# The normalisation of the early groups, dealt out one small piece per step, in two stages of an eight-stage network on one core

## The reference

```python
x = x + _layernorm(_L0_attn_ref(_layernorm(x, axis=-1), ...), axis=-1)   # linear attention, 16 heads
x = x + _layernorm(_L0_ffn_ref(_layernorm(x, axis=-1), ...), axis=-1)
...
x = x + _layernorm(_L2_attn_ref(_layernorm(x, axis=-1), ...), axis=-1)   # causal softmax attention, 16 heads
x = x + _layernorm(_L2_ffn_ref(_layernorm(x, axis=-1), ...), axis=-1)
```

## Time and profile before

| | |
|---|---|
| median of 3 runs | 3116.63 us (3113.25 to 3116.71) |
| the profiled execution | 3116.61 us, span 3114.8 us |
| mean granted TensorE clock | 0.935 of full speed |
| busy: PE | 2705.1 us, 87% of the span |
| busy: DVE | 2057.1 us, 66% |
| busy: ACT | 1571.8 us, 50% |
| busy: POOL | 1074.1 us, 34% |

### The profile page before, as it was taken

How to read it: one execution, slowest core, us unless ns; L and a number is a source line. 1 busy time by engine, 2 the same in 40 slices (tenths; PEclk the granted TensorE clock), 3 DMA queues, 4 the chain that set the end, 5 groups by cost and what they waited for, 6 DMA issues and landing times. The chain is left out here.

```text
span 3114.8 us, 55189 instructions
## 1 busy us (share of the span) xinstructions
PE 2705.1 (87%) x21256; PEld 1691.7 (54%) x21276; DVE 2057.1 (66%) x4308; ACT 1571.8 (50%) x3080; POOL 1074.1 (34%) x784
## 2 busy tenths in 40 slices
PE   8995899989899799998999798798877899777698
PEld 5552455567676566665567566465643334335465
DVE  5758999945644665647554665466548999996554
ACT  4334688862423444444544555365457676643122
POOL 3201000001143344434443444154227777773000
PEclk9995899989899899999999899998999999998899
DMA  1000000001120200000000000000013344340000
GB/s 55 1 4 1 2 3 3 3 2 61 49 92 22 84 1 1 1 1 1 1 1 1 29 1 1 1 1 1 1 52 135 136 143 143 137 141 27 1 1 14
DMA packets 34228, 105.41 MB, mean 34 GB/s; under 512 B 3456, under 2 KB 14592, under 8 KB 33200
## 3 DMA queue, kind: packets, MB, share of 16 engines
q1 hardware_dynamic: 31952, 97.69, 9.0%
q0 software_dynamic: 2016, 4.19, 0.4%
HBM read 94.01 MB, written 7.86 MB: 33 GB/s over the span
## 5 line engine op out<-in xcount | busy, mean ns | idle before, releaser
L2082 POOL TENSOR_TENSOR many_probs<-many_probs,many_rinv 128x2048 f32<-128x2048 f32 (+7 forms) x128 | 269.8, 2107 | 371.6 <-DVE many_rinv L2121 371.6
L1062 DVE TENSOR_REDUCE heads_halfmax<-heads_qmajor 128x1 f32<-128x512 f32 x512 | 316.4, 681 | 32.8 <-PE heads_qmajor L923 29.4
L3477 DVE TENSOR_TENSOR_SCAN stream_state<-stream_decay,stream_state 128x512 f32<-128x512 f32 x256 | 306.3, 1233 | 0.8 <-ACT stream_decay L3309 0.5
L1027 ACT ACTIVATE weights<-heads_kmajor 128x1024 f32<-128x1024 f32 x256 | 259.3, 1027 | 71.7 <-PE heads_kmajor L935 66.3
L2051 ACT ACTIVATE many_probs<-many_score,many_negmax 128x1024 f32<-128x1024 f32 (+7 forms) x256 | 187.4, 737 | 179.7 <-DVE many_negmax L2105 175.9
L2105 DVE TENSOR_REDUCE many_negmax<-many_score 128x1 f32<-128x1024 f32 (+7 forms) x256 | 184.4, 751 | 110.4 <-PE many_score L1980 108.9
L3147 PE MATMUL stream_yacc<-stream_state,ident 128*128 128x512 f32 x512 | 249.1, 614 | 0.4 <-POOL stream_state L3439 0.4
L3309 ACT ACTIVATE stream_decay<-weights,mamba_negA 128x512 f32<-128x512 f32 x256 | 173.0, 689 | 112.5 <-DVE stream_state L3477 111.3
L3439 POOL TENSOR_TENSOR stream_state<-XN,stream_state 128x1024 f32<-128x1024 f32 x85 | 200.4, 2360 | 81.4 <-DVE stream_state L3477 81.1
L1988 PE MATMUL many_ring<-ident,many_probs 128*128 128x128 f32 x1152 | 177.4, 282 | 28.1 <-POOL many_probs L2082 6.5
L3468 DVE TENSOR_TENSOR stream_state<-stream_bspread,stream_du 128x1024 f32<-128x1024 f32 x128 | 153.2, 1197 | 46.5 <-POOL stream_du L3415 38.6
(11 more groups left out here) (585 smaller groups left out, 6023.7 us busy)
## 6 DMA issues: line engine op xcount, KB each, us to landing
XN<-mamba_crows SPq DMA_DIRECT2D x85, 512.0 KB, 3.6
stream_crow<-mamba_crows SPq DMA_DIRECT2D x43, 512.0 KB, 3.6
weights<-in_w_dram SPq DMA_DIRECT2D x1, 6148.0 KB, 17.8
weights<-in_w_dram SPq DMA_DIRECT2D x1, 4274.0 KB, 12.8
weights<-in_w_dram SPq DMA_DIRECT2D x1, 3296.0 KB, 10.7
swiglu_pairs<-swiglu_fetched SPq DMA_DIRECT2D x1, 2310.0 KB, 10.2
weights<-in_w_dram SPq DMA_DIRECT2D x1, 2112.0 KB, 7.9
swiglu_fetched<-swiglu_pairs SPq DMA_DIRECT2D x4, 528.0 KB, 7.3
```

Of the source, the lines that this page charges most:

```text
L1027: nc.scalar.activation(probs_of(k).rearrange("p (a n) -> p a n", a=2), kmajor[:, at:at + 2, :], ACT.Exp, scale=SC).then_inc(exp_done, 1)
L1062: nc.vector.tensor_reduce(halfmax[:, g % 2, at, h % 2:h % 2 + 1], qmajor[:, (2 * n + j) % 3, :], AX, ALU.max).then_inc(max_done, 1)
L2082: nc.gpsimd.tensor_tensor(pair, pair, rinv[:, n % 4, :].unsqueeze(2).broadcast_to([P, 2, wide]), ALU.mult).then_inc(norm_done, 1)
L3477: nc.vector.tensor_tensor_scan(h[:, part(half)], decay[:, (2 * g + half) % DECAYS, :], h[:, part(half)], 0.0 if half == 0 else h[:, BANK - ...
```

## The change

The two group methods `statistics` and `scale` are no longer called in the two stages, nor is `add`; `Normaliser` gets methods for one tile (`statistic`, `scale_tile`, `add_tile`), one for a group's aggregations and variance addition (`merge`), and `batch_step(dve, i)`, which issues what stands in the i-th of 38 places: 8 statistics, 2 merges, a gap of two steps, 2 shifts, a gap, 8 additions, 8 statistics, 2 merges, a gap, 2 shifts. In the linear stage DVE calls it with i = 0 at n = 17 and goes on in the query loop of batch 1 (i = 15 + u); in the 16-head stage with i = n - 70. The scalings on ACT come one per step; in the linear stage those of round 1 stand behind the last query. The roots on POOL move to fitting places.

```diff
+    def statistic(self, dve, k, t):
+        self.wait_added(dve, k, t)
+        self.nc.vector.bn_stats(self.stats[:, k, t, :], self.src[k][:, t, :]).then_inc(self.stat_done[k], 1)
+
+    def merge(self, dve, k, q):
+        for t in range(4 * q, 4 * q + 4):
+            dve.wait_ge(self.stat_done[k], self.count(t))
+            self.nc.vector.bn_aggr(self.mv[:, k, t, :], self.stats[:, k, t, :]).then_inc(self.aggr_done[k], 1)
+        dve.wait_ge(self.aggr_done[k], self.count(4 * q + 3))
+        self.nc.vector.tensor_scalar(self.rstd[:, k, 4 * q:4 * q + 4], self.mv[:, k, 4 * q:4 * q + 4, 1], LN_EPS, None,
+                                     ALU.add).then_inc(self.var_done[k], 1)
+
+    def scale_tile(self, act, k, t):
+        act.wait_ge(self.shift_done[k], self.groups.index(t // 4) + 1)
+        self.wait_added(act, k, t)
+        self.nc.scalar.activation(self.m.XN[:, t, :], self.src[k][:, t, :], ACT.Identity,
+                                  bias=self.shift[:, k, t:t + 1],
+                                  scale=self.rstd[:, k, t:t + 1]).then_inc(self.norm_done[k], 1)
+
+    def add_tile(self, dve, t):
+        self.wait_normalised(dve, 0, t)
+        self.nc.vector.tensor_tensor(self.m.X[:, t, :], self.m.X[:, t, :], self.m.XN[:, t, :],
+                                     ALU.add).then_inc(self.x_added, 1)
+
+    def batch_step(self, dve, i):
+
+        if 0 <= i < 8:
+            self.statistic(dve, 0, i)
+        elif 8 <= i < 10:
+            self.merge(dve, 0, i - 8)
+        elif 12 <= i < 14:
+            self.apply(dve, 0, i - 12)
+        elif 16 <= i < 24:
+            self.add_tile(dve, i - 16)
+        elif 24 <= i < 32:
+            self.statistic(dve, 1, i - 24)
+        elif 32 <= i < 34:
+            self.merge(dve, 1, i - 32)
+        elif 36 <= i < 38:
+            self.apply(dve, 1, i - 36)
...
@@ linear stage, ACT
-                    if n in (23, 24):
-                        nz.scale(act, 0, n - 23)
+                    if n == 31:
+                        nz.scale_tile(act, 0, 0)
                 for u in range(STEPS):
                     query_parts(b, u)
-                    if b == 1 and u in (1, 3):
-                        nz.scale(act, 1, u // 2)
+                    if b == 1 and u < 7:
+                        nz.scale_tile(act, 0, u + 1)
+            for t in range(TPB):
+                nz.scale_tile(act, 1, t)
@@ linear stage, POOL
-                if g in (9, 14):
+                if g == 13:
                     for q in range(2):
-                        nz.root(pool, g // 14, q)
+                        nz.root(pool, 0, q)
+            for q in range(2):
+                nz.root(pool, 1, q)
@@ linear stage, DVE
-                    if n in (17, 18):
-                        dve.wait_ge(y_kept, n - 16)
-                        nz.statistics(dve, 0, n - 17)
-                    if n in (21, 22):
-                        nz.apply(dve, 0, n - 21)
-                    if n in (24, 25):
-                        nz.add(dve, n - 24)
-                    if n in (26, 27):
-                        nz.statistics(dve, 1, n - 26)
-                    if n in (30, 31):
-                        nz.apply(dve, 1, n - 30)
+                    if n == 17:
+                        dve.wait_ge(y_kept, 2)
+                    nz.batch_step(dve, n - 17)
...
+                    if b == 1:
+                        nz.batch_step(dve, 15 + u)
@@ 16-head stage, ACT
-                if n in (78, 80):
-                    nz.scale(act, 0, (n - 78) // 2)
-                if n in (88, 90):
-                    nz.scale(act, 1, (n - 88) // 2)
+                if 83 <= n < 91:
+                    nz.scale_tile(act, 0, n - 83)
+                if 108 <= n < 116:
+                    nz.scale_tile(act, 1, n - 108)
@@ 16-head stage, POOL
-                if n in (75, 85):
-                    for q in range(2):
-                        nz.root(pool, n // 85, q)
+                if n in (79, 80):
+                    nz.root(pool, 0, n - 79)
+                if n in (104, 105):
+                    nz.root(pool, 1, n - 104)
@@ 16-head stage, DVE
-                if n in (70, 72):
-                    dve.wait_ge(act_kept, out_at[0, (n - 70) // 2])
-                    nz.statistics(dve, 0, (n - 70) // 2)
-                if n in (77, 78):
-                    nz.apply(dve, 0, n - 77)
-                if n in (80, 81):
-                    nz.add(dve, n - 80)
-                if n in (82, 83):
-                    nz.statistics(dve, 1, n - 82)
-                if n in (87, 88):
-                    nz.apply(dve, 1, n - 87)
+                if n == 70:
+                    dve.wait_ge(act_kept, out_at[0, 1])
+                nz.batch_step(dve, n - 70)
```

## The result

The changed kernel takes 3094.89 us in the median (3093.39 to 3097.96, 4 runs) against 3114.94 (3110.42 to 3116.71, 4 runs). The ratio is 0.9944 with a 95% interval of 0.9931 to 0.9956, so 13.7 to 21.5 us are gained. The forecast was 3096.6. The profiled execution took 3095.09 us, its span 3093.3. One execution of a later kernel, the linear stage alone, was in a slow state (3925.21 us at a granted clock of 0.637) and is left out of that kernel's figures.

What follows compares the result with a forecast made beforehand. TensorE, busy 87% of the span, was taken as the bound. Linear 7.74 - 0.36 - 0.30 = 7.08 and 16 heads 13.92 - 0.72 - 0.14 - 0.17 = 12.89 gave 19.97: 3116.6 - 20.0 = 3096.6 us, range 3094.0 to 3104.5.

Steps and rivals of the forecast that it cites:

- ceiling of 21.66 us: Most the change could gain: 7.74 us lost in linear batch 1 and 13.92 us over 16-head steps 69 to 93.
- marks and anchors: Marks: POOL's multiplication starts per 16-head step. Anchors: TensorE's first accumulation and first spread product in a linear-stage batch.
- The merges were put at 4 x 0.18: 16-head steps 78, 79, 102, 103: variance addition waits beside POOL's multiplication, 0.72 us in all, bounds 0 and 4.84.
- The scalings at 88 and 112: 16-head stage, ACT: one scaling exceeds its cover by 0.07 us at each of these two steps, 0.14 in all.
- The additions were charged 0.17 once: 16-head stage, DVE: a lone addition lengthens POOL's multiplication by at most 0.17 us, charged in one step; bounds 0 and 1.36.
- The scalings in full query steps: Linear stage, ACT: tiles 5 to 7 need 0.41 us each against 0.31 idle per query step, 0.30 us in all.
- The merges, put at 0.36: Linear stage, first round: two merges behind POOL's running key sum cost 2 x 0.18 us, bounds 0 and 2.11.
- the 2.11 us wait: Linear stage, batch 1: TensorE waits for `lin_key` at 154.65; the clock's fall from 1.00 to 0.52 was called its consequence.
- Rival 1: Only the 16-head stage gains; in the linear stage a wait near 2 us drops the clock again: 3103.7 us, chance 0.12.
- Rival 2: POOL comes first at the additions, steps 86 to 93, holding DVE for whole multiplications; 9.6 us come back: 3106.2, chance 0.10.
- Rival 3: Slower than before: many small waits keep TensorE's clock low in the 16-head stage, 68 us over two cycles: 3165, chance 0.04.
- Rival 4: The change does nothing, the loss being batch 1's or the later pairs' own: 3116.6 us, chance 0.04.

Runs made afterwards that it cites:

- the linear stage alone: The kernel before with the change made only in the linear stage, the 16-head stage as before: median 3108.22 against 3112.11 us, ratio 0.9988.
- The five products: Kernel before plus five unread 128x512 products ahead of batch 1's last accumulation in the linear stage: batch 1 anchors 57.94 us against 60.47, span 3115.2.
- two products in the wait: Kernel before plus two unread 128x512 products ahead of batch 1's last accumulation in the linear stage: batch 1 anchors 59.53 us against 60.47, span 3113.7.

## Why the prediction was right

*The measure.* The step that bore the forecast was to compare each stage with itself, batch 1 with batch 0 and a cycle among the pieces with one free of them. It gave a ceiling of 21.66 us; the marks and anchors gained 13.34 + 7.42 = 20.76 between the two profiles.

*Luck.* The ceiling came from one profile, and the one with the greatest loss in the 16 heads. With the 12.4 us that three of the other four lost (the fourth 11.57) in place of 13.92, the same sum gives a gain of 18.5 us, not 20.0. And the 20.0 were taken from 3116.6 us, while later executions of the kernel before have medians of 3112.11 (15 executions) and 3112.00 (8). That the forecast time came out within 2 us owes something to this; the gain by the ratio, 17.4 us, is less than was foretold.

*Sixteen heads: 12.89 foretold, 13.34 measured.* The merges were put at 4 x 0.18; each pair costs 0.13, since step 78 loses 0.17, gets 0.04 back, and 79 loses nothing though DVE is held for 2.12 us there: the copy is needed only behind TensorE's long score product, which was argued in the prediction and fits, but was not tested by itself. The scalings at 88 and 112 were put at 0.07 each and cost 0.16: the row of four had made the cover seem larger than it was. The additions were charged 0.17 once and cost nothing: the loss at 88 is also there in the run whose additions stand at 96 and 97, so it belongs to ACT. POOL's 3.77 us had not been a price of a lone addition.

*Linear stage: 7.08 foretold, 7.42 measured, 6.3 where the clock falls.* The scalings in full query steps, put at 0.30, cost nothing. ACT's timeline:

```profile
...
162.39 0.49 ACT L183 ACTIVATE XN<-Y,lin_n_shift,lin_n_rstd 128x128 f32<-128x128 f32 x1
162.82 0.60 ACT L617 ACTIVATE lin_featexp<-lin_proj 128x512 f32<-128x512 f32 x1
163.31 0.59 ACT L618 ACTIVATE lin_featrelu<-lin_proj 128x512 f32<-128x512 f32 x1
163.79 0.49 ACT L183 ACTIVATE XN<-Y,lin_n_shift,lin_n_rstd 128x128 f32<-128x128 f32 x1
164.22 0.60 ACT L617 ACTIVATE lin_featexp<-lin_proj 128x512 f32<-128x512 f32 x1
...
```

An exponential, a relu and a scaling follow one another every 1.40 us (162.82 to 164.22), which is TensorE's own cycle. A span of 0.60 us gives way after 0.49, so the idle 0.31 of the earlier trace rows understates the room: the next instruction can start earlier than its predecessor's span ends. The merges, put at 0.36, cost nothing at the accumulation; what is left, 53.05 - 52.74 = 0.31, arises behind it. From 151.22 to 173.86 TensorE takes 22.64 us where batch 0 takes 22.32. All of it is there at the key sums: they start 153.48 - 151.22 = 2.26 us behind the accumulation, in batch 0 59.48 - 57.44 = 2.04, and take 1.95 in place of 1.84. POOL's timeline shows why they start late:

```profile
...
141.89 2.35 POOL L650 TENSOR_TENSOR lin_keytotal<-lin_keytotal,lin_key 128x1024 f32<-128x1024 f32 x1 [3.02 <-DVE lin_key L668]
144.19 2.66 POOL L225 TENSOR_TENSOR lin_n_rstd<-lin_n_rstd,neghalf 128x4 f32<-128x4 f32 x2
146.83 2.34 POOL L650 TENSOR_TENSOR lin_keytotal<-lin_keytotal,lin_key 128x1024 f32<-128x1024 f32 x1
151.07 2.36 POOL L650 TENSOR_TENSOR lin_keytotal<-lin_keytotal,lin_key 128x1024 f32<-128x1024 f32 x1 [1.90 <-DVE lin_key L668]
...
```

The sum of group 13 starts 21.08 us behind the anchor where its like in batch 0 starts at 20.43, the two roots then take all of POOL's idle time, and the last sum ends at 151.07 + 2.36 = 153.43, 0.05 us ahead of the key sums. So the merges and the roots together do cost 0.22 us, by way of the running sum; why the key sums then take 0.11 us longer stays open. The prediction had put the roots at nothing, with the late sum named and left in the bound.

*The clock.* The prediction calls the fall a consequence of the 2.11 us wait. The five products show that TensorE, kept at work there, keeps the full clock, and that the steps behind are then as fast as in batch 0; they took POOL's wait away as well, so that the one wait alone is the cause is not shown. What the prediction lacked is that the clock can fall in the changed stage too, and with no wait ahead of it. Rival 1, of 0.12, spoke of such a fall behind a wait near 2 us; the fall came in some executions, at about a quarter of its former price.

*The rivals.* Rival 1 is out, the linear stage gained 6 to 7 us. Rival 2 is out, the additions came first; its mechanism is real. Its price of 9.6 us was not tested: with three of the eight held for long it was 1.00 us. Rival 3 is out: the marks hold the cycle with the clock at 1.00. Rival 4 is out.

*What stays open.* Rows of additions, statistics and scalings, put back one kind at a time, cost about 5.2, 2.5 and 3.3 us (the scalings 1.15 in round 0, and in round 1, by steps 88 and 90 of the kernel before, 1.30 + 0.96 less one lone scaling of 0.16). If they simply add, that is with the 0.6 of the changed kernel 11.5 of the 11.6 to 13.9 us that the kernel before lost. How much of each is waiting and how much the clock was not separated. Neither is it known why the clock falls behind the key sums in some executions only. The ratio's 17.4 us is less than the 21.5 between the two first profiles; the first one of the kernel before had the greatest loss of five in the 16 heads.

## What to carry to other kernels

Where a stage runs the same loop with and without extra work, subtract the two: it gives the ceiling of any re-placing before a single cost is known. Spread extra work in pieces shorter than the smallest idle time of the engine, right behind the instruction that starts POOL, so that a DVE instruction with two SBUF inputs comes first. And look behind a wait of TensorE for a fall of the clock and price it too: here that was 3.8 us or more, next to a wait of 2.11. Take the ceiling from more than one profile: here it varied by 2.35 us.

## What the runs showed of the hardware

- An addition of two SBUF tiles, 0.27 us alone, was held until 0.14 us after the end of POOL's operation in three cases out of three, and was not held in the changed kernel's eight steps, where it came 0.16 us ahead of POOL's start, nor where it found POOL idle. This agrees with the Trainium skill, page "SBUF — State Buffer", section "Who interferes with whom": the first to issue keeps the shared ports for the whole instruction.
- The variance addition has one SBUF input of four elements and is held all the same (2.12 us beside a 2.32 us multiplication), while statistics and aggregations of the same engine are not: in the kernel before, four aggregations took 0.36 us while POOL was at its 1.47 us multiplication (at 1404.14), as they do beside an idle POOL. The same section says that a `tensor_scalar` can enter a mode that takes both ports, where its operands allow it; the wait in the trace agrees with that, the mode itself no run shows.
- Beside a wait of 2.11 us the granted clock fell from 1.00 to about 0.5 for some 10 us. It fell too, to 0.75 and 0.57, where the waits were only 0.40 and 0.68 us (two products in the wait). And in the second profile of the changed kernel it fell to 0.77 behind the key sums, although TensorE's timeline shows no wait between 140 and 165 us, while the first profile of the same program has 1.00 there. So a fall can come with no wait ahead of it; what decides it is not shown.
